# Other step distances in the expert blocks of an RWKV and mixture-of-experts kernel, and 16 places for the rows of a block

## The reference

```
x = x + layernorm(rwkv(layernorm(x)))       # three projections, WKV recurrence along T, output projection
x = x + layernorm(moe(layernorm(x)))
moe(h): probs = softmax(h @ router_w); the best 2 of 8 experts per token, weights topw
        routed = sum over the 2 of topw * (silu(h @ w1[e]) @ w2[e])         # 256 -> 256 -> 256
        shared = sigmoid(h @ shared_gate_w) * ((silu(gate) * up) @ shared_down)
        result = routed + shared
```

## Time and profile before

| | |
|---|---|
| median of 3 runs | 1617.3 us (1615.18 to 1617.86) |
| span of the profiled execution, first to last instruction | 1700.2 us; the page gives no other time for this execution |
| PE busy | 1531.9 us, 90% |
| DVE / ACT / POOL busy | 1387.4 / 1332.3 / 1058.5 us |
| first turning of a block | at 1095.25 us |
| first addition of pass 1, of pass 2 | at 1116.36 and 1391.06 us |
| last scatter begins | at 1690.75 us |

### The profile page before, as it was taken

One profiled execution on the slowest core, in us unless ns is written; L12 is line 12 of the kernel. 1 busy time (PEld: TensorE's weight loads), 2 busy tenths in 40 slices (PEclk: granted clock), 3 DMA queues, 4 the chain that ended last, 5 costly groups with the idle time before them and its releaser, 6 DMA issues.

```text
span 1700.2 us, 35246 instructions
## 1 busy us (share of the span) xinstructions
PE 1531.9 (90%) x9960; PEld 1367.7 (80%) x9960; DVE 1387.4 (82%) x3139; ACT 1332.3 (78%) x2768; POOL 1058.5 (62%) x1167
## 2 busy tenths in 40 slices
PE   4889999999999999999999996689898888888882
PEld 3778888888888888888888885579898888878782
DVE  4798998999998999999998986467666668888883
ACT  3788988988988998998988986456565568888883
POOL 1156677667667677676676666635564536666665
PEclk8999999999999999999999997889999989999997
DMA  4113223223223223223223212587786645666661
GB/s 118 38 52 101 90 77 114 90 77 114 80 75 101 78 78 101 79 77 101 81 75 101 68 66 98 199 257 244 240 268 201 198 138 157 191 187 199 196 196 43
DMA packets 122316, 214.42 MB, mean 126 GB/s; under 512 B 19975, under 2 KB 62730, under 8 KB 122128
## 3 DMA queue, kind: packets, MB, share of 16 engines
q1 hardware_dynamic: 90064, 126.13, 25.2%
q0 software_dynamic: 32064, 86.04, 13.9%
HBM read 116.37 MB, written 99.39 MB: 127 GB/s over the span
## 4 chain that ended last, share of the span: by engine, by line
PE 63%; issue 8%; DVE 8%; ACT 6%; another core or an unknown queue 4%; POOL 3%; SPq 1%; DMA 1%; DVEq 1%; ACTq 1%; POOLq 0%
PE PS L1483 44%; PE PS L1701 6%; PE PS L1717 5%; PE PS L1475 3%; PE PS L1682 3%; POOL d_xd L575 2%; PE PS L1547 2%; PE PS L1545 1%; ACT al L966 1%; ACT h2h L970 1%; DVE rkl L1455 1%; POOL out L639 1%; DVE rkl L1453 1%; ACTq L959 1%
## 5 line engine op out<-in xcount | busy, mean ns | idle before, releaser
L575 POOL DMA_INDIRECT d_xd<-h2n,ixs x248 | 310.7, 1253 | 201.4 <-DVE h2n L1210 133.9
L1483 PE MATMUL PS<-hTh,wqh 128*128 128x512 f32 x768 | 306.4, 399 | 15.2 <-ACT kk L676 10.0
L1483 PE MATMUL PS<-hTh,wql 128*128 128x512 f32 x768 | 305.9, 398 | 0.0
L1483 PE MATMUL PS<-hTl,wqh 128*128 128x512 f32 x768 | 305.8, 398 | 0.0
L1483 PEld LDWEIGHTS PS<-hTh,wqh 128*128 128x128 f32 x768 | 146.4, 191 | 49.9 <-ACT kk L676 10.9
L1483 PEld LDWEIGHTS PS<-hTh,wql 128*128 128x128 f32 x768 | 145.9, 190 | 34.5
L1483 PEld LDWEIGHTS PS<-hTl,wqh 128*128 128x128 f32 x768 | 146.4, 191 | 33.4
L582 POOL DMA_INDIRECT d_xs<-ysh,ixs x124 | 132.3, 1067 | 46.1 <-issue 46.1
L1701 PE MATMUL PS<-rkh 128*128 128x256 f32 x284 | 86.3, 304 | 56.1 <-DVE rkl L1455 36.8
L1461 DVE TENSOR_TENSOR h2l<-al,h2h 128x512 fp32r<-128x512 f32 x95 | 65.5, 690 | 69.4 <-ACT h2h L970 49.0
L1717 PE MATMUL PS<-weh,h2h 128*128 x380 | 107.7, 283 | 0.7 <-issue 0.6
(11 more groups left out here) (327 smaller groups left out, 5701.2 us busy)
## 6 DMA issues: line engine op xcount, KB each, us to landing
xin<-in_L_attn_x SPq DMA_DIRECT2D x32, 512.0 KB
x<-in_L_attn_x SPq DMA_DIRECT2D x32, 512.0 KB
wqh<-d_xd SPq DMA_DIRECT2D x60, 272.0 KB
wql<-d_xd SPq DMA_DIRECT2D x60, 272.0 KB
d_xd<-ee SPq DMA_DIRECT2D x18, 272.0 KB
wel<-in_L_ffn_w SPq DMA_DIRECT2D x16, 256.0 KB
d_xd<-h2n,ixs POOLq DMA_INDIRECT x248
kk<-d_xs SPq DMA_DIRECT2D x12, 256.0 KB
```

The costliest lines, as they stand in the source:

```text
L575: g.indirect_dma_start(d_xd[s], bass.IndirectOffsetOnAxis(ap=ixs[:, m % 2, k:k + 1], axis=0), h2n_of(m)[:, j, :], None).then_inc(s_sct[s], 16)
L1483: ins = mm_(out_ap, l, r, start=(k == 0), stop=(k == len(todo) - 1))
```

## The change

The distances become: PE first product of t-2, second product of t-5; ACT silu of t-3, squares and rows of t-7; DVE low part of the hidden values t-3, addition t-6, `back` t-8, scaling t-9. Turned rows and first weights get a third buffer each (the third weight buffer is the old output matrix `woh`/`wol`, which the blocks don't need). `xb` has 16 places instead of 12: the old projection, gate and down weights now lie in one tensor, so that more places fit; block 14 and 15 wait until the last `down` product is done. The first partial results are loaded behind block 6 of pass 1 (five at once) as before, and behind block 9 of pass 2 (eight at once).

```
-    NX = NYB = 12
+    NX, NYB = 16, 12
     LY = 2
-    LT = 6
+    LTS = (6, 9)
+    ROWS_HELD = max(LTS) + 1
...
-        xTh = [hTh[:, 0, 0:TC], rkh[:, 0, :]]
-        xTl = [hTl[:, 0, 0:TC], rkl[:, 0, :]]
+        xTh = [hTh[:, 0, 0:TC], rkh[:, 0, :], hTh[:, 1, 0:TC]]
+        xTl = [hTl[:, 0, 0:TC], rkl[:, 0, :], hTl[:, 1, 0:TC]]
...
-        w1h = [shh[:, 1, :], rkh[:, 1, :]]
-        w1l = [shl[:, 1, :], rkl[:, 1, :]]
+        w1h = [shh[:, 1, :], rkh[:, 1, :], flat(woh)]
+        w1l = [shl[:, 1, :], rkl[:, 1, :], flat(wol)]
... SP
+                if b == 14:
+                    sp.wait_ge(s_dn, n(NCH - 1, 2, 2))
...
-                if b == LT - 2:
+                if b == LTS[0] - 2:
                     shared_tails(ends)
...
-                due = [b - LY] if LY <= b < NB + LY and (b - LY) % NB1 >= LT - LY else []
-                if b % NB1 == LT and b < NB:
-                    due = list(range(b - LT, b - LY + 1))
+                due = [b - LY] if b >= LY and (b - LY) % NB1 >= LTS[(b - LY) // NB1] - LY else []
+                if b < NB and b % NB1 == LTS[b // NB1]:
+                    due = list(range(b - LTS[b // NB1], b - LY + 1))
... ACT
-            for t in range(NB + 4):
+            for t in range(NB + 7):
...
-                    if t >= 2:
-                        act.wait_ge(s_hid, t - 1)
-                    copy(xTh[t % 2], PS[t % 2][:, :]).then_inc(s_xh, 1)
+                    if t >= 3:
+                        act.wait_ge(s_hid, t - 2)
+                    copy(xTh[t % 3], PS[t % 2][:, :]).then_inc(s_xh, 1)
...
-                u = t - 1
+                u = t - 3
...
-                if t - 4 >= NB1:
-                    last_squares(t - 4 - NB1)
-                    back_second(t - 4 - NB1)
+                if t - 7 >= NB1:
+                    last_squares(t - 7 - NB1)
+                    back_second(t - 7 - NB1)
... DVE
-                u = t - 1
+                u = t - 3
...
-                if 0 <= t - 3 < NB:
-                    y_out(t - 3)
-                if 0 <= t - 3 - NB1 < NB1:
-                    back(t - 3 - NB1)
-                if t - 6 >= NB1:
-                    final(t - 6 - NB1)
+                if 0 <= t - 6 < NB:
+                    y_out(t - 6)
+                if 0 <= t - 8 - NB1 < NB1:
+                    back(t - 8 - NB1)
+                if t - 9 >= NB1:
+                    final(t - 9 - NB1)
... PE
-                if 0 <= t - 1 < NB:
+                if 0 <= t - 2 < NB:
...
-                    block_hidden(t - 1)
+                    block_hidden(t - 2)
...
-                    block_out(t - 3, e)
+                w = t - 5
...
+                    block_out(w, e)
```

More of the change, by code:

```diff
@@ L73, in rwkv_moe @@
         wel = sb("wel", [P, E * 1024], F32R)
-        wqh = sb("wqh", [P, 3, 2, H, D], F32R)
-        wql = sb("wql", [P, 3, 2, H, D], F32R)
+        wah = sb("wah", [P, 18 * D], F32R)
+        wal = sb("wal", [P, 18 * D], F32R)
+        wqh, wql = [t[:, 0:12 * D].rearrange("p (q s a n) -> p q s a n", q=3, s=2, a=H) for t in (wah, wal)]
+        wgh, wgl = [t[:, 12 * D:16 * D].rearrange("p (a n) -> p a n", a=H) for t in (wah, wal)]
+        wdh, wdl = [t[:, 16 * D:18 * D].rearrange("p (a n) -> p a n", a=H) for t in (wah, wal)]
         woh = sb("woh", [P, H, D], F32R)
         wol = sb("wol", [P, H, D], F32R)
[L78 to L81, removed]
         rwf = sb("rwf", [P, H, RW])
@@ L330, in rows @@
             return flat(t).rearrange("p (j d) -> p j d", j=NT)
[L333 to L336, removed]
+        xb = [t[:, i * 2 * XW:(i + 1) * 2 * XW].bitcast(F32).rearrange("p (j d) -> p j d", j=2)
+              for places in ((0, 1, 2, 3, 4), (5, 6), (7,)) for t in (wah, wal) for i in places]
         sil = [flat(t)[:, i * 2 * D:(i + 1) * 2 * D] for t, i in ((al, 0), (be, 0), (al, 1))]
@@ L452, in load_block @@
                 r = sp.value_load(tabx[0:1, s, b % NB1:b % NB1 + 1], min_val=0, max_val=E * CAP)
-                first_row[b % (LT + 1)] = r
+                first_row[b % ROWS_HELD] = r
                 sp.dma_start(xb[b % NX], d_xd[s][bass.ds(r, BLK), :].rearrange("(p j) d -> p j d", p=P)
@@ L461, in load_result @@
                 rows_in = d_xs if w < NB1 else d_ys
-                sp.dma_start(yb[w % NYB], rows_in[bass.ds(first_row[w % (LT + 1)], BLK), :].rearrange("(p j) d -> p j d", p=P)
+                sp.dma_start(yb[w % NYB], rows_in[bass.ds(first_row[w % ROWS_HELD], BLK), :].rearrange("(p j) d -> p j d", p=P)
                              ).then_inc(s_yl[w % NYB], 16)
@@ L955, in _ @@
                     act.wait_ge(s_Tx, t + 1)
-                    if t >= 2:
-                        act.wait_ge(s_hid, t - 1)
-                    copy(xTh[t % 2], PS[t % 2][:, :]).then_inc(s_xh, 1)
+                    if t >= 3:
+                        act.wait_ge(s_hid, t - 2)
+                    copy(xTh[t % 3], PS[t % 2][:, :]).then_inc(s_xh, 1)
                     base = act.value_load(tabp[0:1, t // NB1, t % NB1:t % NB1 + 1], min_val=0, max_val=(E - 1) * 1024)
-                    copy(w1h[t % 2], weh[:, bass.ds(base, H * D)]).then_inc(s_w1h, 1)
-                u = t - 1
+                    copy(w1h[t % 3], weh[:, bass.ds(base, H * D)]).then_inc(s_w1h, 1)
+                u = t - 3
                 if 0 <= u < NB:
@@ L1433, in final @@
                                            in1=xk[v % 4][:, j, :], op0=ALU.mult, op1=ALU.add).then_inc(s_fin, 1)
-            for t in range(NB + 6):
+            for t in range(NB + 9):
                 if t == 9:
@@ L1450, in _ @@
                     dve.wait_ge(s_xh, t + 1)
-                    if t >= 2:
-                        dve.wait_ge(s_hid, t - 1)
-                    V.tensor_tensor(xTl[t % 2], PS[t % 2][:, :], xTh[t % 2].bitcast(F32), ALU.subtract).then_inc(s_xl, 1)
+                    if t >= 3:
+                        dve.wait_ge(s_hid, t - 2)
+                    V.tensor_tensor(xTl[t % 3], PS[t % 2][:, :], xTh[t % 3].bitcast(F32), ALU.subtract).then_inc(s_xl, 1)
                     base = dve.value_load(tabp[0:1, t // NB1, t % NB1:t % NB1 + 1], min_val=0, max_val=(E - 1) * 1024)
-                    V.tensor_copy(w1l[t % 2], wel[:, bass.ds(base, H * D)]).then_inc(s_w1l, 1)
-                u = t - 1
+                    V.tensor_copy(w1l[t % 3], wel[:, bass.ds(base, H * D)]).then_inc(s_w1l, 1)
+                u = t - 3
                 if 0 <= u < NB:
@@ L1692, in block_hidden @@
                     pe.wait_ge(s_sil, u - 2)
-                xh, xl, wh, wl = xTh[u % 2], xTl[u % 2], w1h[u % 2], w1l[u % 2]
+                xh, xl, wh, wl = xTh[u % 3], xTl[u % 3], w1h[u % 3], w1l[u % 3]
                 for f in range(2):
@@ L1718, in block_out @@
                 ins.then_inc(s_yp, 1)
-            for t in range(NB + 3):
+            for t in range(NB + 5):
                 if t < NB:
                     block_in(t)
-                if 0 <= t - 1 < NB:
-                    if t == 1:
+                if 0 <= t - 2 < NB:
+                    if t == 2:
                         pe.wait_ge(s_ys, n(NCH - 1, NT, NT))
-                    block_hidden(t - 1)
-                if t - 3 == NB1:
+                    block_hidden(t - 2)
+                w = t - 5
+                if w == NB1:
                     pe.wait_ge(s_tab, 5)
-                if t >= 3:
-                    e = pe.value_load(tabp[0:1, (t - 3) // NB1, (t - 3) % NB1:(t - 3) % NB1 + 1], min_val=0, max_val=(E - 1) * 1024)
-                    block_out(t - 3, e)
+                if w >= 0:
+                    e = pe.value_load(tabp[0:1, w // NB1, w % NB1:w % NB1 + 1], min_val=0, max_val=(E - 1) * 1024)
+                    block_out(w, e)
 _VECTORS = ["L0_attn_time_decay", "L0_attn_time_first", "L0_attn_time_mix_k", "L0_attn_time_mix_v",
```

## The result

| | before | after |
|---|---|---|
| median (fastest and slowest run) | 1617.2 us (1615.2 to 1618.1, 6 runs) | 1625.1 us (1622.7 to 1632.8, 6 runs) |
| ratio, 95% interval | | 1.005 (1.0037 to 1.0063): slower by 7.9 us |
| span of the profiled execution | 1700.2 us; of a second one (first experiment) 1614.3 us | 1623.4 us; of a second one 1622.9 us |

I forecast 1618.5 us and no change that can be told; the time is inside the range and 6.6 us above the forecast. In one later comparison the changed kernel took 1627.6 us against 1617.6, ratio 1.0056 (1.0032 to 1.0081). Single runs at 1634 to 1642 us occur in experiments 2 and 8 too; no trace caught one, so their cause is open.

The account below looks back on a forecast made before the run. Taken as bound: PE at 3.27 us a step in pass 1, four engines within 5% in pass 2 (3.43). Terms +1.8 + 2.5 - 1.65 - 0.15 - 1.3 = +1.2 us; forecast 1618.5 us, range 1596 to 1626.

Parts of the forecast that it names:

- 16 places: Block rows in pass 2: 15 places usable, rows asked for about four steps ahead as before; 0.
- rival C: Switch between passes: longer chain and block 81 late behind eight loads make it slower, 1622.5 us; chance 0.25.
- Budget, late releases: Both passes: waits on late releases belong to the profiled execution; without them the span would be 1611.8 us.
- Start and more work ahead: Pass 1: start -0.5 us, two more turnings and one more first product before block 70's second product +2.3; together +1.8.
- switch: Pass 1 to pass 2: chain through DVE, POOL and SP to the first addition gets longer, +2.5 us.
- From there to the first scaling: Start of pass 2, first addition to end of first scaling: 9.25 us instead of 10.9, -1.65.
- PE's gap: Switch between passes: PE waits 2.7 us before (4.26 in the profile) and doesn't wait after.
- Eight loads ahead of block 81: Pass 2: block 81, loaded behind eight partial results, arrives just in time; 0, at worst +1.5 us.
- Steady steps: Steps between start and end: engines may be further apart, -1.3 us, bounds 0 and -5.5.
- Drain: End of pass 2: nine blocks instead of six scaled after the last turning, at 3.38 instead of 3.43 us; -0.15.
- PE's clock: Switch: PE's clock may fall behind its gap before; counted 0, bound -2.3 us.
- look at block 81 and at loads in pass 1: Where to look for the cause if the time rises by over 5 us.

Follow-up runs that it names:

- first experiment: The kernel before, unedited, run and traced a second time: 1616.1 us, span 1614.3 us.
- experiment 2: Changed kernel, but SP asks for the partial result of block b-4 instead of b-2 behind the rows of block b: 1619.0 us, ratio 1.0014.
- experiment 8: Against experiment 2: pass 2 reads rows of `d_xd` in place of `d_ys`, without waiting for pass 1's last scatters: 1617.6 us, ratio 1.0005.
- experiment 7: Changed kernel with every distance behind the first product one step less (second product four, addition five, scaling eight): 1618.5 us, ratio 0.9985.
- Experiment 10: Experiment 2 with 15 places for block rows instead of 16, rows still asked for ahead of the partial result: 1621.6 us, ratio 1.0043.
- experiment 4: Changed kernel with the step distances of before, keeping 16 places and three buffers for rows and weights: 1619.9 us, ratio 1.0005.
- experiment 12: Experiment 2 with shorter distances behind the first product: second product, addition and `back` four, squares five, scaling seven: 1615.0 us, ratio 0.9981.
- twelve places: Changed kernel with its new distances, but 12 places for block rows as before: 1825.4 us, ratio 1.1272.
- experiment 3: Changed kernel with the addition moved to the head of DVE's step: 1633.2 us, ratio 1.0092.
- experiment 5: Changed kernel with the addition first in DVE's step and the partial result of block b-4 asked for behind block b: 1640.2 us, ratio 1.0128.
- experiments 9: Changed kernel, unedited, run and traced again: 1627.6 us, ratio 1.0056.

## Why the prediction missed

**The step that failed** is "*16 places.* ... block rows are asked for about four steps ahead in pass 2, as before. 0." The count of 15 places was right, and so was "as before". The four steps were not: in before, taken again, the request stands in the mean 7.8 us ahead of DVE's low part of the block, which is 2.3 steps. And the price of 0 had no working behind it: I never set the steps against what they have to hold. That 1625.1 lies inside the range of 1596 to 1626 is luck, since its upper end was drawn for rival C, and late rows stood at nothing. The chain of before, taken again, for block 114 (its place was block 102's), from DVE, POOL, SP, PE, ACT and DVE:

```profile
1466.12 0.88 DVE L1432 SCALAR_TENSOR_TENSOR kk<-kk,rsw,xin 128x256 f32<-128x256 f32 x2
...
1471.20 1.02 POOL L639 DMA_INDIRECT out<-kk,wql  x1 [0.31 <-issue]
...
1475.73 0.34 SPq L454 DMA_DIRECT2D wql<-d_xd  x1
...
1481.28 0.60 PE L1682 MATMUL PS<-ident,wql 128*128 128x128 f32 x4
...
1482.79 0.57 ACT L958 CAST hTh<-PS 128x512 fp32r<-128x512 f32 x1
...
1484.12 0.68 DVE L1453 TENSOR_TENSOR hTl<-PS,hTh 128x512 fp32r<-128x512 f32 x1
```

From scaling to second scatter 5.1 us (5.4 in the mean), to the request 4.5 (4.7 in the median); rows are usable about 3.5 us behind their request (the page's medians to landing are 3.5 and 3.7), and from turning to low part are at least 1.3. Within the step DVE comes to the scaling 2.65 us behind the low part. Together 17.6 us, and they have to fit into (places in use - scaling distance) steps of 3.44:

| kernel | places in use - distance | room, us | body, us |
|---|---|---|---|
| before | 12 - 6 | 20.6 | 238.5 |
| after | 15 - 9 | 20.6 | 246.0, 243.5 |
| results four behind | 16 - 9 | 24.1 | 237.8 |
| one less | 15 - 8 | 24.1 | 237.5 |
| fifteen places, rows first | 15 - 9 | 20.6 | 237.7 |
| places only; scaling seven | 15 - 6; 16 - 7 | 31.0 | 237.9; 237.9 |
| before with 11 places | 11 - 6 | 17.2 | 258.6 |
| twelve places | 12 - 9 | 10.3 | 441.4 |

The last two rows are past the edge: 258.6 / 70 = 3.69 us a block x 5 = 18.5, and 441.4 / 70 = 6.31 x 3 = 18.9, so the chain takes 18.5 to 19 us when it binds. Before and after both have 1.6 to 3 us to spare. In after SP's request of the partial result stands 1.1 us ahead of the rows' own (before has the rows first), and from scatter to request are 5.2 us instead of 4.7. The rows take longer, too, when the partial result is asked for first. Where the traces show the landing of a row load of pass 2 (of 55 loads, 18 to 31 in the first group and 7 to 23 in the second), its median is 3.6 to 4.1 us behind the request in after, after taken again and experiments 4 and 7, and 3.0 to 3.2 in before and experiments 2, 10 and 12, which ask for the rows first. So the order lengthens after's chain by about 1.1 us, to 18.7, and leaves 1.9 of the 3 us to spare. That puts it nearer to the edge, where one slow load is enough. Experiment 10's runs leave open how much of the time between two kernels with the same room this order makes. Single times of before reach 1630.2 us as well; whether its rhythm broke in them, no trace shows.

What one slow load does, the timelines show. In after the rows of block 98 were usable 5.2 us behind their request, and PE and ACT slipped (SP, PE and ACT):

```profile
1413.99 0.34 SPq L452 DMA_DIRECT2D wah<-d_xd  x1
...
1419.21 0.66 PE L1682 MATMUL PS<-ident,wah 128*128 128x128 f32 x4 [1.69 <-DMA wah<-d_xd]
...
1419.90 0.59 ACT L958 CAST hTh<-PS 128x512 fp32r<-128x512 f32 x1 [0.76 <-PE PS L1682]
```

DVE lost 0.7 us, and POOL met DVE's steps at another place. POOL's norms and one of its scatters from there on:

```profile
1419.16 1.04 POOL L633 TENSOR_TENSOR rsw<-varw,mh 128x4 f32<-128x4 f32 x1
...
1426.91 1.04 POOL L633 TENSOR_TENSOR rsw<-varw,mh 128x4 f32<-128x4 f32 x1
...
1434.85 1.16 POOL L633 TENSOR_TENSOR rsw<-varw,mh 128x4 f32<-128x4 f32 x1
1436.21 1.77 POOL L639 DMA_INDIRECT out<-vv,wah  x1 [0.20 <-issue]
...
1443.60 1.37 POOL L633 TENSOR_TENSOR rsw<-varw,mh 128x4 f32<-128x4 f32 x1
...
1452.34 1.04 POOL L633 TENSOR_TENSOR rsw<-varw,mh 128x4 f32<-128x4 f32 x1
```

Two blocks take POOL 7.75, 7.94, 8.75 and 8.74 us instead of 6.88, because its scatters take up to 1.77 us instead of 1.02 to 1.21. Places come free late by the sum, and nine blocks behind the first slip, from 107 on, DVE loses most of what it loses; it begins with the 1.2 us for which DVE waits for POOL's norm in the view of waits above. The second execution repeats it: a slip at block 122, norms at 1504.92, 1512.50, 1520.48, 1529.24 and 1537.98, and the large loss at 131 to 133, nine on. After its slip at block 94 POOL recovered. So the price of a late row seems to be set less by PE's wait than by what it does to POOL's rhythm; no experiment separates the two. That the order of DVE's step sets what POOL's norm takes is shown by experiments 3 and 5; that POOL's scatters grow by the same cause is read from the traces only.

**The other terms**, in absolute time of the traces of before, taken again, and after:

- *Budget, late releases.* Right: I put the span of a normal execution at 1611.8, and it was 1614.3.
- *Start and more work ahead*, +1.8, *switch* +2.5: first addition of pass 2 forecast 4.3 later, measured 1351.50 - 1347.85 = 3.65. Right within 0.7. By part, the end of block 70's second product came 0.9 later instead of 1.8, and from there to pass 2's first addition are 11.7 us instead of 8.9, so +2.8; I had 10.0 and 7.5. Both were too short because I read the chain from block 70's addition as 6.5 us: it is 1391.06 - 1382.68 = 8.4 in the earlier trace rows, with 1.9 between the addition and POOL's first scatter, which I left out. And DVE's wait for the first partial result, which I had shorter by two, is 4.84 against 5.04: the chain starts with the addition of block 70, and that moves as well, by 3.85.
- *From there to the first scaling*, -1.65, 9.25 us: the ends are 10.5 us apart (1351.50 to 1361.14 and 0.87), before 12.5, so -2.0. The difference was right; both lengths were 1.3 to 1.6 too short, because DVE waits twice for ACT there.
- *PE's gap* before pass 2 goes: right, 4.19 us before (I had 2.7 for a timed run, by the same short chain), 1.15 at one second product after.
- *Eight loads ahead of block 81*: PE waited 0.64 us there. 0 was right in its effect on DVE.
- *Steady steps*, -1.3: where rows are in time the body is 237.5 to 237.9 against 238.5, so -0.6 to -1.0. But experiment 4, with the distances of before, has 237.9 as well, so none of it comes from the distances: 0 instead of -1.3. Undisturbed steps are 3.44 us. There was nothing to win, since DVE was already busy in 50.00 of 50 us.
- *Drain*, -0.15: from the last low part to the last scaling are 30.6 us after and 20.4 before, so three more blocks take 3.41 us each instead of 3.44, -0.1. Right. *PE's clock*: the granted clock of 1350 to 1400 is 1.00 after and 0.97 before, PE isn't the bound there, 0.
- Rival C had the sign and, with 1622.5, nearly the time, by a mechanism that the runs put at 1.7 of the 9.1 us. Its sum was off, too: taken from the forecast, with nothing won in the steady steps, it is 1618.5 + 1.3 + 1.5 = 1621.3. My note "look at block 81 and at loads in pass 1" pointed to the wrong pass.

## What to carry to other kernels

In a pipeline whose input places are freed by its last stage, write down (places - distance of the last stage) x step and set it against the whole chain from that stage back to the first, norm, scatter, landing, request and load: a distance that lengthens the one must bring its own places. Add one step of reserve beyond "it just fits": with it 4 of 47 runs took over 1623 us (experiments 2, 7, 8 and 12, the four in 2 and 8), without it 13 of 24 (experiments 9 and 10). Lengthen only the distance that removes a wait (here the first product's), and let what stands behind it keep the gaps that it had: that version (experiment 12, with the reserve) is faster than both kernels.

## What the runs showed of the hardware

- One profiled execution can be 5% longer than another of the same kernel (1700.2 against 1614.3 us, where no timed run of it took more than 1630.3), with waits of over 2 us on releases in both passes that no other execution had.
- POOL's 128x4 power takes 1.04 us where it begins under a DVE operation that reads PSUM, and 1.87 us where it begins with a copy and a subtraction of SBUF tensors; its indirect DMAs take 0.97 to 1.77 us. POOL has so little room (6.88 us for two blocks, nearly all of it busy or issuing) that the order of DVE's step alone makes it the bound: moving one DVE operation cost 7 us by the ratios in experiment 3, and 18 in experiment 5 against experiment 2 (22 in the body of pass 2). Which resource the two engines meet at is not shown.
- Of a load of 272 KB, usable about 3.5 us behind its request, single ones take 5.2 us (after, before taken again, experiment 4) or 5.6 (experiment 7). Asked for behind a load of 256 KB instead of ahead of it, the rows land about 0.6 us later.
